# Two of 25 products added by a DMA transfer instead of by TensorE, in a deformable convolution

## The reference

```python
x = x + dcnv4(groupnorm(x), ...)        # layer 0
x = x + binary_conv3x3(groupnorm(x), ...)  # layer 1
# dcnv4: G = 32 groups of GC = 8 channels, 9 taps
xdw = depthwise3x3(x) + dw_b
om = xdw @ om_w + om_b                   # per group and tap: two offsets, one mask
value = x @ vp_w + vp_b
sampled = bilinear samples of value at (pixel + tap + offset)
out = sum over taps of sampled * mask
return out @ op_w
```

## Time and profile before

| | us |
|---|---|
| Median of 3 runs | 3860.18 |
| Lowest and highest of 3 runs | 3853.02, 3861.33 |
| The profiled execution's own time | 3859.76 |
| Its span, first to last instruction | 3858.0 |
| PE matmuls busy | 3628.5 (94%) |
| PE weight loads busy | 2369.5 (61%) |
| DVE busy | 3510.0 (91%) |
| ACT busy | 2286.0 (59%) |
| POOL busy | 565.0 (15%) |
| Mean DMA rate | 122 GB/s |

### The profile page before, as it was taken

How to read it: one execution, slowest core, us unless ns; L and a number is a source line. 1 busy time by engine, 2 the same in 40 slices (tenths; PEclk the granted TensorE clock), 3 DMA queues, 4 the chain that set the end, 5 groups by cost and what they waited for, 6 DMA issues and landing times. The chain is left out here.

```text
span 3858.0 us, 90635 instructions
## 1 busy us (share of the span) xinstructions
PE 3628.5 (94%) x37696; PEld 2369.5 (61%) x37696; DVE 3510.0 (91%) x2757; ACT 2286.0 (59%) x4547; POOL 565.0 (15%) x412
## 2 busy tenths in 40 slices
PE   4899999999999999999999999999999999858998
PEld 2566666666666666666666666666666666623333
DVE  4899999999999999999999999989999999948776
ACT  5556665666666665666556666665566666235554
POOL 0011111101111111111111001111111111104444
PEclk9999999999999999999999999999999999979999
DMA  6454565445555555455545555555544554345563
GB/s 177 100 111 102 110 125 132 101 111 116 124 120 109 114 123 115 94 108 127 131 99 119 112 121 114 107 122 131 118 100 97 106 107 94 52 158 199 209 215 147
DMA packets 319939, 470.35 MB, mean 122 GB/s; under 512 B 37244, under 2 KB 242684, under 8 KB 313736
## 3 DMA queue, kind: packets, MB, share of 16 engines
q0 software_dynamic: 94080, 196.11, 28.4%
q1 hardware_dynamic: 224584, 266.07, 23.2%
q10 hardware_dynamic: 832, 2.10, 0.1%
HBM read 262.53 MB, written 67.41 MB: 86 GB/s over the span
## 5 line engine op out<-in xcount | busy, mean ns | idle before, releaser
L1026 DVE TENSOR_TENSOR pv<-val,wsum 128x2048 f32<-128x2048 f32 x800 | 1811.2, 2286 | 21.4 <-ACT xdw L557 14.6
L796 PEld LDWEIGHTS ps_add<-ident,pv 128*128 128x128 f32 x12800 | 1401.2, 142 | 356.0 <-issue 223.7
L796 PE MATMUL ps_add<-ident,pv 128*128 128x128 f32 x12800 | 1527.2, 275 | 70.9 <-DVE pv L1026 62.7
L751 PE MATMUL ps_om<-xdw,omw 128*32 128x256 f32 x13824 | 868.4, 384 | 30.4 <-ACT hat L587 29.4
L585 ACT ACTIVATE hat<-ps_om,omb 128x256 f32<-128x256 f32 x576 | 276.0, 479 | 551.2 <-PE ps_om L751 501.9
L979 DVE TENSOR_TENSOR prod<-hat,mwy 128x1536 f32<-128x1536 f32 (+1 forms) x384 | 526.0, 1397 | 82.9 <-DMA wsum<-prod 61.8
L472 POOL DMA_DIRECT2D wsum<-prod x192 | 226.0, 1254 | 2556.8 <-DVE wsum L979 2556.8
L751 PEld LDWEIGHTS ps_om<-xdw,omw 128*32 128x32 f32 x13824 | 391.2, 109 | 330.2 <-issue 95.5
L589 ACT ACTIVATE msk<-ps_om,omb 128x256 f32<-128x256 f32 x288 | 137.0, 476 | 401.4 <-PE ps_om L751 399.3
L965 DVE TENSOR_TENSOR mwy<-hat,msk 128x768 f32<-128x768 f32 x288 | 274.4, 953 | 94.3 <-ACT hat L599 94.3
L722 PE MATMUL ps_bg<-tri,diag 128*32 128x512 f32 x3024 | 346.5, 592 | 11.9 <-ACT tri L551 11.9
(11 more groups left out here) (134 smaller groups left out, 2622.7 us busy)
## 6 DMA issues: line engine op xcount, KB each, us to landing
wsum<-prod POOLq DMA_DIRECT2D x160, 768.0 KB, 7.1
tri<-in_x_dram SPq DMA_DIRECT2D x725, 128.0 KB, 2.9
win<-in_x_dram SPq DMA_DIRECT2D x144, 256.0 KB, 3.6
x<-xres SPq DMA_DIRECT2D x128, 256.0 KB, 5.1
xres<-in_x_dram POOLq DMA_DIRECT2D x124, 256.0 KB, 8.4
out_dram<-c_x SPq DMA_DIRECT2D x31, 1024.0 KB, 4.5
c_x<-x SPq DMA_DIRECT2D x30, 1024.0 KB, 5.3
c_box<-box_d SPq DMA_DIRECT2D x16, 1024.0 KB, 7.4
```

The lines of the kernel that those rows point to most:

```text
L751: mm = nc.tensor.matmul(ps_om[G * q:G * q + G, (par + i) % 2, 0:TOK], omw[:, h, comp, :], xdw[:, j % 2, h, q, :], start=h == 0, stop=h == ...
L796: mm = nc.tensor.matmul(ps_add[:, tb, c, :], pv[:, (j + uv) % PBUF, c, P * tb:P * tb + P], consts["ident"][:, :], start=uv == 0 and c % 4 ...
L1026: nc.vector.tensor_tensor(pv[:, (j + uv) % PBUF, :, :].rearrange("p c (r w) -> p c r w", w=W), val[:, :, SR * j + u:SR * j + u + SR, v:v + ...
```

## The change

Product 0 is no longer added by PE. When DVE has made products 0 and 1, POOL starts one accumulating transfer that adds the buffer of product 0 to that of product 1 (`add_pair`, 1 MB, SBUF to SBUF). PE then adds the buffer of product 1 once, so 24 buffers in place of 25. In PE's order no product is added at k=4 any more; at k=5 product 2 comes in the early place, and 1 and 3 in the late one. The first product of a sum is now product 2. DVE's multiply of product 4, which reuses the buffer of product 0, waits for the transfer in place of PE, and that of product 5 for PE's addition of product 1, as before. POOL's transfer stands in its queue behind that of tap 3 and ahead of the load at k=6 and the transfer of tap 6.

```diff
--- before.py
+++ after.py
@@ -37,6 +37,11 @@
 PIECES = 4
 SAMPLES_AT = [(13, 14, 15), (16, 17, 18), (19, 20, 21), (22, 23, 24), (0, 1), (2, 3), (4, 5, 6), (7, 8, 9), (10, 11, 12)]
 SAMPLED = 4
+PAIRED = {1: 0}
+PAIRS = list(PAIRED)
+ADDS_AT = [(13, 14, 15), (16, 17, 18), (19, 20, 21), (22, 23, 24), (), (2, 1, 3), (4, 5, 6), (7, 8, 9), (10, 11, 12)]
+ADDED = [uv for k in (4, 5, 6, 7, 8, 0, 1, 2, 3) for uv in ADDS_AT[k]]
+ADDS = len(ADDED)
 SENT_TAPS = (1, 2, 3, 6, 7)
 GROUP = C // 32
 KROWS, CB = 3 * 32, P // 32
@@ -262,6 +267,7 @@
         mwy_done, prod_done, wadd_done = sem("mwy_done"), sem("prod_done"), sem("wadd_done")
         wsum_added = sem("wsum_added")
         pv_full, add_done, add_out = sem("pv_full"), sem("add_done"), sem("add_out")
+        pair_added = sem("pair_added")
         xres_added, stats2 = sem("xres_added"), sem("stats2")
         gn_kept = sem("gn_kept")
         x_ahead = [sem("x_ahead0"), sem("x_ahead1")]
@@ -472,11 +478,21 @@
                         nc.gpsimd.dma_start(wsum[:, ky + a:ky + b, kx + c:kx + d, :], in_prod((a, b, c, d)), accum_op=ALU.add)\
                             .then_inc(wsum_added, 16)
 
+                def add_pair(n, j, uv):
+
+                    s = STEPS * n + j
+                    pool.wait_ge(pv_full, SHIFTS * s + uv + 1)
+                    at_least(pool, pair_added, 16 * (len(PAIRS) * s + PAIRS.index(uv)))
+                    nc.gpsimd.dma_start(pv[:, (j + uv) % PBUF, :, :], pv[:, (j + PAIRED[uv]) % PBUF, :, :],
+                                        accum_op=ALU.add).then_inc(pair_added, 16)
+
                 for n in range(NI):
                     for j in range(STEPS):
                         for k in SENT_TAPS:
-                            if k == 6 and j < CH and n < NI - 1:
-                                load_ahead(n, j, 0, "back3")
+                            if k == 6:
+                                add_pair(n, j, 1)
+                                if j < CH and n < NI - 1:
+                                    load_ahead(n, j, 0, "back3")
                             add_products(n, j, k)
                         if j < CH and n < NI - 1:
                             load_ahead(n, j, 1, "project3")
@@ -601,7 +617,7 @@
 
                 def summed(s):
 
-                    act.wait_ge(add_done, SHIFTS * (s + 1))
+                    act.wait_ge(add_done, ADDS * (s + 1))
                     for tb in range(TB):
                         last = nc.scalar.activation(acc[:, tb, :, :, :].rearrange("p q c g -> p c q g"),
                                                     ps_add[:, tb, :, :].rearrange("p c (q g) -> p c q g", q=Q), ACT.Copy)
@@ -787,15 +803,18 @@
                                      start=True, stop=True).then_inc(bg_full, 2)
 
                 def add(s, j, uv):
-                    pe.wait_ge(pv_full, SHIFTS * s + uv + 1)
-                    if uv == 0:
+                    if uv in PAIRED:
+                        pe.wait_ge(pair_added, 16 * (len(PAIRS) * s + PAIRS.index(uv) + 1))
+                    else:
+                        pe.wait_ge(pv_full, SHIFTS * s + uv + 1)
+                    if uv == ADDED[0]:
                         at_least(pe, add_out, s)
                     for tb in range(TB):
                         for c in range(GC):
 
                             mm = nc.tensor.matmul(ps_add[:, tb, c, :], pv[:, (j + uv) % PBUF, c, P * tb:P * tb + P],
-                                                  consts["ident"][:, :], start=uv == 0 and c % 4 == 0,
-                                                  stop=uv == SHIFTS - 1, is_transpose=True, skip_group_check=True)
+                                                  consts["ident"][:, :], start=uv == ADDED[0] and c % 4 == 0,
+                                                  stop=uv == ADDED[-1], is_transpose=True, skip_group_check=True)
                     mm.then_inc(add_done, 1)
 
                 pe.wait_ge(mean_loaded, 16)
@@ -815,11 +834,14 @@
                     s = STEPS * n + j
                     n1, j1 = following(n, j)
 
-                    def add_next(k, i):
-                        if k < SAMPLED and not first:
-                            add(s - 1, j - 1, SAMPLES_AT[k][i])
-                        elif k >= SAMPLED and i < len(SAMPLES_AT[k]):
-                            add(s, j, SAMPLES_AT[k][i])
+                    def add_next(k, early):
+
+                        before = [uv for uv in ADDS_AT[k][:1] if uv not in PAIRED]
+                        for uv in before if early else ADDS_AT[k][len(before):]:
+                            if k >= SAMPLED:
+                                add(s, j, uv)
+                            elif not first:
+                                add(s - 1, j - 1, uv)
 
                     def place(name):
                         return unit(n, j, name, NI), bank(n, j, name, NI)
@@ -834,7 +856,7 @@
                         if ahead_of:
                             offsets(*ahead_of, 0)
                             offsets(*ahead_of, 1)
-                        add_next(k, 0)
+                        add_next(k, True)
                         if ahead_of:
                             offsets(*ahead_of, 2)
                         if k in DW_AT and not last:
@@ -853,14 +875,13 @@
                             for u in range(PJ_UNITS):
                                 if PROJECT_AT[u] == k:
                                     project(u, *place(f"project{u}"), unit(n, j, "back3", NI))
-                        add_next(k, 1)
-                        add_next(k, 2)
+                        add_next(k, False)
 
                 for n in range(NI):
                     for j in range(STEPS):
                         step(n, j, (n, j) == (0, 0), (n, j) == (NI - 1, STEPS - 1))
                 for k in range(SAMPLED):
-                    for uv in SAMPLES_AT[k]:
+                    for uv in ADDS_AT[k]:
                         add(STEPS * NI - 1, STEPS - 1, uv)
                 at = unit(NI - 1, STEPS - 1, "project3", NI) + 1
                 for u in range(BACK_UNITS):
@@ -1019,8 +1040,11 @@
                         dve.wait_ge(wsum_added, 16 * (sent_before(TAPS) * s + sent_before(k + 1)))
                     else:
                         dve.wait_ge(wadd_done, (TAPS - 1 - len(SENT_TAPS)) * s + kept_before(k + 1))
-                    if not isinstance(s, int) or s > 0 or uv >= PBUF:
-                        dve.wait_ge(add_done, SHIFTS * s + uv - PBUF + 1)
+                    used, in_step = (uv - PBUF, s) if uv >= PBUF else (uv - PBUF + SHIFTS, s - 1)
+                    if used in PAIRED.values():
+                        dve.wait_ge(pair_added, 16 * (len(PAIRS) * in_step + list(PAIRED.values()).index(used) + 1))
+                    elif not isinstance(s, int) or in_step >= 0:
+                        dve.wait_ge(add_done, ADDS * in_step + ADDED.index(used) + 1)
                     w_in = wsum[:, u, v, :].rearrange("p (r w) -> p r w", w=W).unsqueeze(1)\
                         .to_broadcast([P, GC, SR, W])
                     nc.vector.tensor_tensor(pv[:, (j + uv) % PBUF, :, :].rearrange("p c (r w) -> p c r w", w=W),
```

## The result

The changed kernel takes 3849.22 us (median of 14 executions, 3845.42 to 3853.65), the one before 3860.07 us (14 executions on the same chips, 3853.02 to 3864.41). The ratio is 0.9974, with a 95% interval from 0.9965 to 0.9982: 10.9 us or 0.26% faster. The profiled executions show the same: 3848.84 us after, 3859.76 us before, and spans of 3847.0 and 3858.0 us.

What follows compares the result with a forecast made beforehand. DVE was taken as the bound nearly everywhere, PE leading only at image boundaries. Six boundaries at -1.5 us plus 0.5 at the seventh gave -8.5, so 3859.8 became 3851.3 us (chance 0.47); range 3835 to 3866.

Steps and rivals of the forecast that it cites:

- DVE is bound, PE decides only at the image boundaries: Layer 0: DVE leads nearly everywhere, PE only around j=3 and the following j=0; at most 50.7 us of waits can go.
- Product 0's removal gives 0.8 us, not 1.9: At k=4 on PE: offsets part 2 must still wait for ACT, so PE gains only 0.8 us a step.
- The transfer lands 9.9 us after product 1: POOL's 1 MB transfer: landing within 8.45 to 11.3 us, ahead of product 4 and PE's addition at 12.6, so cost 0.
- the rival: Transfer lands late, DVE waits at product 4 every step: 3896 us at 14 us, 3864 at 13; chance 0.16.
- The new wait at product 5: DVE waits for PE's later addition of product 1: 3.0 us in j=3, 1 to 2 us in j=0.
- a wait in j=1 or j=2: Sign that the forecast is wrong: product 5 waiting in these steps, where 1.1 us to spare was expected.
- The `hat` waits vanish and tap 7's transfer appears: DVE's waits for ACT fall from 44 us to under 10; a `wsum` wait of about 1.8 us appears in each j=3.
- -1.5 us a boundary: Net change in DVE's time at an image boundary, from a range of -1.2 to -2.0 us, counted at six of seven.
- The exception that was made for the boundary at 2600 us: One of seven boundaries: nothing won in j=0, about 0.5 us of the loss in j=3 stays.
- All waits go: Rival: PE is far less behind than thought, boundaries lose their waits on PE, about -4.5 us each: 3829 us; chance 0.13.
- The gain doesn't reach DVE: Rival: turning back at k=4 hangs on ACT, the 0.8 us is lost, -3 us in all: 3857 us; chance 0.24.
- PE's relief worth nothing: Rival reading from weight loads' 94.67 us busy against matmuls' 140.17: PE is not the bound, 3860 us; no separate chance.

Runs made afterwards that it cites:

- The late transfer: The changed kernel with POOL's transfer waiting for product 3 in place of product 1: 4014.1 us, ratio 1.0402 to the kernel before the change.
- both pairs: Against the kernel before the change: products 0 and 1, and 10 and 11, paired by transfers, product 1 added ahead of the projection: 3846.81 us, ratio 0.9966.

## Why the prediction was right

The forecast's sum was 3851.3 us, from its main case; 3849.22 was measured. The page's two groups of PE that the change touches, before and after (times, then busy us, mean ns, idle time before and what ended it):

```profile
L796 PE MATMUL ps_add<-ident,pv 128*128 128x128 f32 x12800 | 1527.2, 275 | 70.9 <-DVE pv L1026 62.7
L751 PE MATMUL ps_om<-xdw,omw 128*32 128x256 f32 x13824 | 868.4, 384 | 30.4 <-ACT hat L587 29.4
```

```profile
L815 PE MATMUL ps_add<-ident,pv 128*128 128x128 f32 x12288 | 1464.0, 276 | 68.6 <-DVE pv L1050 68.1
L767 PE MATMUL ps_om<-xdw,omw 128*32 128x256 f32 x13824 | 869.6, 384 | 71.8 <-ACT hat L603 70.8
```

The steps one by one:

- **DVE is bound, PE decides only at the image boundaries: right.** The line of PE's additions fell by 63 us (1527.2 to 1464.0), where 61 was worked out. All of PE fell by only 52.9, because its groups overlap in time where one follows on another: taken group by group the busy time falls by 60.5 (3782.4 to 3721.9), and 7.6 us of that was overlap. The time fell by 11, of which 10.3 arose between the marks at the boundaries.
- **Product 0's removal gives 0.8 us, not 1.9: right.** 0.86 by the two PE rows of the example, 1.26 us of wait on ACT where 1.3 was expected (41.4 more over the kernel, in these rows), and the pair of runs that take out product 0 (0.87 us less on PE) or product 6 (1.75 us less).
- **The transfer lands 9.9 us after product 1: mis-sized, without effect.** It lands after 7.2 to 9.5 us. The whole of 8.45 us at the transfer of 768 KB was scaled half by size; from issue to landing, 1 MB takes 7.6 us at the median and 768 KB takes 7.0. The margin was therefore larger than thought: 3.1 to 5.4 us in place of 1.3 to 4.1. PE came to product 1 at least 3.9 us after the landing, but only 0.8 us after it in the very first step. The late transfer costs what the rival said, once it is really late. The rival's reason that it shares a queue with SP's loads was a misreading: the page has the 33.6 MB more in q0 (196.11 and 229.66 MB), where POOL's transfers are, and q1 unchanged at 266.07 MB.
- **The new wait at product 5: right in place and size.** In j=3 it is 21.1 us over seven steps, 3.0 each, as forecast. In j=0 it is 7.0 us in five of seven steps, 0.9 to 2.0. The total of the row, 29.9, is the forecast's "about 30". Three waits of 0.5 to 0.7 us in j=2, 1.6 in all, weren't foreseen: in its fastest steps PE comes to product 1 13.0 us after it and not 12.6, so 0.4 of the 1.1 us to spare wasn't there. The prediction had named a wait in j=1 or j=2 as a sign that it is wrong; in three of 16 such steps there is one; by its own sign that part failed, at a cost too small to matter.
- **The `hat` waits vanish and tap 7's transfer appears: right.** No `hat` wait of layer 0 is left in the list (below 10 was forecast). In j=3 the transfer's wait is 8.9 us in six steps, 1.5 each, where 1.8 was said.
- **-1.5 us a boundary: right as a mean, not in each, and in part by luck.** Single boundaries run from +0.3 to -3.1 us, as other transfer waits shift with them. The run without the transfer, which has the same order on PE, gave -7.1 at the seven boundaries (a mean of -1.0) and -11.3 over layer 0, so one trace fixes the mean to about half a microsecond, not to a tenth. The exception that was made for the boundary at 2600 us, +0.5, was wrong: it gave -2.4, because the loss in j=3 was won back at the `hat` waits right behind it as elsewhere. The sum was -8.5. From product 1 of the first step to the last product of layer 0, all of DVE's idle time fell by 8.3 us (140.1 to 131.8); its busy time fell by 2.7 (3125.1 to 3122.4), which the sum didn't have and these rows don't explain. Layer 1 gave nothing: the difference is -11.2 us at layer 0's last product and -11.0 in the span.
- **The rivals.** "All waits go" is out by the wait at product 5. "The gain doesn't reach DVE" asked for 3857, above every one of the 14 executions. PE's relief worth nothing (3860, from the weight loads' time) is out by the run without product 6: 0.5% from 16 matmuls a step, with DVE's own work unchanged. The prediction drew this rival from the Trainium skill (Trainium Kernel Development and Optimization, Performance Expectations), which calls matmul busy time a bad metric for how close a kernel is to roofline; that says nothing of which engine the others wait for, and the trace settled it by DVE's waits.

What stays open: why the run without the transfer (3852.95) has a higher median than with it. Their intervals overlap, so it may be no difference. Of the expectations for more gain, the one that missed by most (both pairs at 3835, 12 us too low) fell to the five stops at the jumps and to product 15's wait; with both out of the way, 3833.69 was measured.

## What to carry to other kernels

Work taken from an engine pays where another engine waits for it, and there only as far as no third engine's chain stands in parallel: look for the place first (16 matmuls at k=6 gave 21 us, at k=4 beside ACT's chain 16). When an addition is delayed to make room, look who reuses its buffer; the wait that appears may only replace another, and then its price is the order on the engine that is late, not the wait's length. Moving the delayed piece ahead of a block that itself waits for ACT gave nearly as much again as the change. And after each edit look at the first instruction behind a loop's jump back, and at what the DMA queues carry there.

## What was not expected of the hardware

- An accumulating transfer of 1 MB within SBUF takes 7.6 us to land against 7.0 us for one of 768 KB. A third more bytes cost 9% more time, so most of it doesn't grow with the size, as far as two sizes cut into different pieces can tell.
- A jump back in DVE's loop leaves DVE idle for 0.1 to 0.5 us in seven kernels and for 3.8 us in two others, with loops of nearly the same length (540 or 544 instructions, and 544). The instruction packet behind the jump starts 3.6 us later in those two, where a 1 MB transfer is under way. The stop is no one's wait by semaphore and shows as "issue".
